# Bias tables beside the first image, tail loads on ScalarE's queue, image sums every two pairs

## What is computed

```
x = x + windowed_attention(group_norm(x))         # windows of 8x8, shifted by 4; 8 heads; relative bias table
t = tokens(x)                                      # 1024 a image
t = t + banded_attention(layer_norm(t))            # windows of 128 tokens, band of 32; 4 heads
t = t + experts(layer_norm(t))                     # top 2 of 8 experts: gelu(x W1 + b1) W2 + b2
```

## Time and profile before

| what | us |
|---|---|
| median of 3 runs | 3270.21 |
| lowest and highest run | 3255.96 and 3283.94 |
| the profiled execution | 3266.06 |
| its span, first to last instruction | 3264.20 |
| passes end, last pairs begin (about) | 2828 |

### The profile page before, as it was taken

The page is one execution under the profiler, slowest core; times in us unless marked ns, Lnnn a source line. Parts: engine busy times, 40 slices in busy tenths (PEclk is TensorE's granted clock), DMA queues, the critical chain, the costliest instruction groups (busy, mean ns, idle before and its releaser), DMA issues.

```text
span 3264.2 us, 76818 instructions
## 1 busy us (share of the span) xinstructions
PE 2561.1 (78%) x27338; PEld 1806.2 (55%) x27338; DVE 1947.2 (60%) x5091; ACT 1863.9 (57%) x3409; POOL 1778.5 (54%) x2054
## 2 busy tenths in 40 slices
PE   3888888888888888788999888989888777545460
PEld 1455555556666666566666666666665555434340
DVE  2467777777666666767666776667766655312122
ACT  1576565566776677567766777777766554212120
POOL 0335555555444444666666666666677775443336
PEclk9899999998999999899999999999998888778775
DMA  3343333433444544334334353343433344444543
GB/s 110 117 159 115 116 114 112 158 147 130 152 158 167 174 162 143 106 92 121 121 121 121 95 157 109 113 117 117 137 120 111 109 130 122 140 126 153 160 146 91
DMA packets 262426, 421.97 MB, mean 129 GB/s; under 512 B 41741, under 2 KB 141081, under 8 KB 261281
## 3 DMA queue, kind: packets, MB, share of 16 engines
q1 hardware_dynamic: 229280, 349.88, 32.3%
q0 software_dynamic: 32768, 67.17, 7.3%
HBM read 198.26 MB, written 231.22 MB: 132 GB/s over the span
## 4 chain that ended last, share of the span: by engine, by line
PE 30%; ACT 9%; issue 8%; another core or an unknown queue 4%; POOL 4%; DVE 4%; SPq 1%; DMA 1%; ACTq 0%; POOLq 0%; DVEq 0%
PE bank_m L824 6%; PE bank_m L817 4%; POOL yg L1215 2%; PE bank_to L751 2%; PE bank_s L706 2%; PE bank_s L719 2%; PE bank_s L745 1%; PE bank_s L797 1%; PE bank_s L791 1%; PE bank_to L760 1%; ACT pt_sb_a L1035 1%; ACT v_a L1020 1%; ACT L1162 1%; PE bank_s L729 1%
## 5 line engine op out<-in xcount | busy, mean ns | idle before, releaser
L1215 POOL DMA_INDIRECT yg<-y_sorted,place_i x512 | 511.9, 1000 | 434.2 <-DMA out_dram<-yg 119.7
L1205 POOL DMA_INDIRECT x_sorted<-xn_c,place_i x512 | 532.3, 1040 | 322.2 <-PE bank_s L690 121.2
L1198 POOL TENSOR_TENSOR s_sb_a<-s_sb_a,mx_a 128x512 f32<-128x512 f32 x256 | 266.9, 1043 | 614.4 <-DVE mx_a L1557 608.8
L1549 DVE TENSOR_TENSOR s_sb_a<-bank_s,bias_a 128x512 f32<-128x512 f32 x256 | 176.7, 690 | 447.9 <-PE bank_s L690 267.2
L817 PE MATMUL bank_m<-xe,wk_e 128*128 128x512 f32 x552 | 277.3, 627 | 62.8 <-ACT hid L1068 46.0
L824 PE MATMUL bank_m<-wk_e,hid 128*128 128x128 f32 x2208 | 290.8, 296 | 3.3 <-ACT hid L1068 3.3
L824 PEld LDWEIGHTS bank_m<-wk_e,hid 128*128 128x128 f32 x2208 | 285.3, 212 | 4.4 <-issue 4.3
L1198 POOL TENSOR_TENSOR s_sb_b<-s_sb_b,mx_b 128x512 f32<-128x512 f32 x256 | 269.4, 1052 | 23.8 <-DVE mx_b L1557 23.6
L1035 ACT ACTIVATE pt_sb_b<-bank_to 128x512 f32<-128x512 f32 x256 | 152.6, 596 | 207.1 <-PE bank_to L751 127.2
L1189 POOL TENSOR_TENSOR km_a<-qk_a,k_consts 128x128 f32<-128x128 f32 x512 | 207.7, 429 | 79.3 <-DVE qk_a L1401 74.7
L1068 ACT ACTIVATE hid<-bank_m,wk_e 128x512 f32<-128x512 f32 x276 | 182.3, 686 | 94.5 <-PE bank_m L817 62.3
(11 more groups left out here) (220 smaller groups left out, 6053.4 us busy)
## 6 DMA issues: line engine op xcount, KB each, us to landing
y_sorted<-t_back SPq DMA_DIRECT2D x192, 512.0 KB
wk_e<-in_w_experts_dram SPq DMA_DIRECT2D x156, 321.0 KB
y_sorted<-yo SPq DMA_DIRECT2D x170, 256.0 KB
xs<-x_sorted SPq DMA_DIRECT2D x156, 256.0 KB
t_kept<-t SPq DMA_DIRECT2D x64, 256.0 KB
t_back<-t_kept SPq DMA_DIRECT2D x32, 512.0 KB
xin<-in_x_dram SPq DMA_DIRECT2D x128, 112.0 KB
x_res<-in_x_dram SPq DMA_DIRECT2D x256, 56.0 KB
```

The costliest lines, as they stand in the source:

```text
L1198: pool.tensor_tensor(s[:, :, :], s[:, :, :], m[:, :, None].to_broadcast(shape), ALU.subtract).then_inc(s_sub[w], 1)
L1205: pool.indirect_dma_start(out=x_sorted[group_of[d] % XSIDES].ap(), out_offset=bass.IndirectOffsetOnAxis(ap=place_i[:, d, n:n + 1], axis=0) ...
L1215: pool.indirect_dma_start(out=yg[:, c % 2, n, :], out_offset=None, in_=y_sorted[side].ap(), in_offset=bass.IndirectOffsetOnAxis(ap=place_i ...
L1549: tt(s_sb[0][:, :, :].rearrange("p (r h) n -> p r (h n)", h=2), scores, bias_a[:, kind, :, :].rearrange("p (r h) n -> p r (h n)", h=2), AL ...
```

## The change

Three things are changed.

1. The start. The loads are split: six that the table needs (`table_loads`, semaphore `table_loaded`) come first, then the first image, then the 14 others (`loads`, semaphore `loaded`). SyncE sends the table out and back ahead of the 12 zero stores. TensorE no longer waits for `ready` or for the table's return; the 16 unfolding matmuls are done in two halves inside pass -1, at t = 4 behind the keys' projection and at t = 5 behind the squared norms. VectorE splits the rows behind step 5 of pass -1 and makes the four tables behind its step 7. TensorE waits for both in step 0 of pass 0, behind its first scores. The banks that the table uses in PSUM are others.
2. The loads of the tail. From pair 2 of the tail on, `load_pair` is called by ScalarE, behind the Gelus of pair n and the copy of pair n+1, instead of by SyncE ahead of the store of pair n.
3. `PAIRS_PER_SUM` is 2.0: images 20 to 27 are summed behind pairs 2, 4, 6, 8, 10, 14, 16 and 18, and 28 to 31 late.

The core of the diff:

```diff
-PAIRS_PER_SUM = 2.5
+PAIRS_PER_SUM = 2.0
...
+        table_loads = [(tab_s, rel_table), (cw1_s, cpb_w1), (cb1_s[:], cpb_b1),
+                       (cw2_s[:], cpb_w2.rearrange("(c p) n -> p c n", p=P)), (fold_s, unfold), (k[:], consts)]
+        loads = [(wq_s[:], wq), (wk_s[:], wk), (wv_s[:], wv), (wo_s[:], wo),
...
+        def load_pair(eng, u):
...
             load_image(0)
+            for dst, src in loads:
+                sp.dma_start(dst, src).then_inc(loaded, 16)
+            sp.wait_ge(setup, RELS)
+            sp.dma_start(scratch.ap(), rel_s).then_inc(bias_io, 16)
+            sp.wait_ge(bias_io, 16)
+            unfolded = bass.AP(scratch, 0, [[1, WS], [REL, HA * REL], [1, WS]])
+            sp.dma_start(unf_s, unfolded).then_inc(bias_io, 16)
             sp.wait_ge(blank, 1)
             for side in range(XSIDES):
...
-            sp.wait_ge(setup, 9)
-            sp.dma_start(scratch.ap(), rel_s).then_inc(bias_io, 16)
...
             for n, u in enumerate(tail):
-                if n + 2 < len(tail):
-                    load_pair(tail[n + 2])
                 store_pair(u)
...
# TensorE
-            pe.wait_ge(loaded, 16 * len(loads))
+            pe.wait_ge(table_loaded, 16 * len(table_loads))
...
-            pe.wait_ge(ready, 3)
+            pe.wait_ge(loaded, 16 * len(loads))
+            mm(T[:, 0:P], cols[:, 2:3].to_broadcast([P, P]), wo_s[:], start=True, stop=True).then_inc(rows_split, 1)
+
+            def unfold_table(rows):
+
+                pe.wait_ge(bias_io, 32)
+                for py in rows:
+                    last = mm(bank_m[:, 0, :].rearrange("p (h n) -> p h n", h=HA), fold_s[:, py * P:py * P + P],
+                              unf_s.rearrange("p (h y) w -> p h (y w)", h=HA)[:, :, py * WS:py * WS + WTOK],
+                              start=(py == 0), stop=(py == WS - 1))
+                if rows[-1] == WS - 1:
+                    last.then_inc(setup, 1)
...
+                if n == 0:
+                    pe.wait_ge(rows_split, SPLIT)
+                    pe.wait_ge(setup, BIASED)
...
+                if t == 4 and i == -1:
+                    unfold_table(range(0, WS // 2))
                 if t == 5 and on(f):
                     squared_norms(f, (0, 1))
+                if t == 5 and i == -1:
+                    unfold_table(range(WS // 2, WS))
# ScalarE, the tail
                 if n + 1 < len(tail):
                     slots_copy(pairs[tail[n + 1]], tail_banks[(n + 1) % 4])
+                if n >= 0 and n + 2 < len(tail):
+                    load_pair(act, tail[n + 2])
# VectorE
+            def output_rows():      # the split of two rows, as before, on rows_split
...
+            def window_bias():
+
+                dve.wait_ge(setup, UNFOLDED)
+                for kind in range(4):
+                    a = CONST["mask_a"][0] + kind * WTOK
+                    last = tt(bias_a[:, kind, :, :], bank_m[:, 0, :].rearrange("p (h n) -> p h n", h=HA),
+                              k[:, None, a:a + WTOK].to_broadcast([P, HA, WTOK]), ALU.add)
+                last.then_inc(setup, 1)
+                dve.wait_ge(setup, BIASED)
...
             for i in range(-1, PASSES):
                 for t in range(TILES):
                     step(i, t)
+                    if i == -1 and t == 5:
+                        output_rows()
+                if i == -1:
+                    window_bias()
```

More of the change, by code:

```diff
@@ L443, in hybrid_kernel @@
                  (row_b, b_proj.to_broadcast([P, P])), (bo_s, bo.to_broadcast([P, P])),
[L444 to L445 removed]
+                 (gb_s[:], gate_b.to_broadcast([P, E]))]
+        RELS, UNFOLDED, BIASED, SPLIT = 7, 8, 9, 17
+        def load_pair(eng, u):
+            pair = pairs[u]
+            side, tiles = pair.group % XSIDES, table[pair.group % 2]
+            if u == 0 or pairs[u - 1].group != pair.group:
+                eng.wait_ge(tabled, TABLE_STEPS * (pair.group + 1))
+                eng.wait_ge(scattered, 16 * TOP * TILES * (last_image[pair.group] + 1))
+                eng.wait_ge(zeroed, 16 * (SPARE_DMAS + E * pair.group))
+                zeros = x_sorted[side].ap()[E * REGION:E * REGION + SLOTS, :].rearrange("(p j) d -> p (j d)", p=P)
+                for e in range(E):
+                    row = eng.value_load(tiles[0:1, 2 * MAX_TILES + e:2 * MAX_TILES + e + 1],
+                                        min_val=0, max_val=BUFFER - SLOTS)
+                    rows = x_sorted[side].ap()[bass.ds(row, SLOTS), :].rearrange("(p j) d -> p (j d)", p=P)
+                    eng.dma_start(rows, zeros).then_inc(zeroed, 16)
+                eng.wait_ge(zeroed, 16 * (SPARE_DMAS + E * (pair.group + 1)))
+            for m, q, kth in pair.members:
+                b = buffer_of(q)[0]
+                after(eng, yo_ready, q - (3 if q < TAIL_FIRST else 5))
+                if b >= 4:
+                    eng.wait_ge(s_ready[0], IMAGES * TILES)
+                    eng.wait_ge(km_ready, IMAGES * TILES)
+                row = eng.value_load(tiles[0:1, kth:kth + 1], min_val=0, max_val=BUFFER - SLOTS)
+                expert = eng.value_load(tiles[0:1, MAX_TILES + kth:MAX_TILES + kth + 1], min_val=0, max_val=E - 1)
+                rows = x_sorted[side].ap()[bass.ds(row, SLOTS), :].rearrange("(p j) d -> p (j d)", p=P)
+                eng.dma_start(xs_b[b], rows).then_inc(tile_in[b], 16)
+                weights = w_experts[bass.ds(expert, 1), :, :].rearrange("e p n -> (e p) n")
+                eng.dma_start(wk_b[b], weights).then_inc(tile_in[b], 16)
@@ L464, in load_residual @@
                                      x_rolled[a, r, c0:c1, tiles, :]).then_inc(xr_in[h], 16)
[L466 to L486, removed]
-                    row = sp.value_load(tiles[0:1, kth:kth + 1], min_val=0, max_val=BUFFER - SLOTS)
-                    expert = sp.value_load(tiles[0:1, MAX_TILES + kth:MAX_TILES + kth + 1], min_val=0, max_val=E - 1)
-                    rows = x_sorted[side].ap()[bass.ds(row, SLOTS), :].rearrange("(p j) d -> p (j d)", p=P)
-                    sp.dma_start(xs_b[b], rows).then_inc(tile_in[b], 16)
-                    weights = w_experts[bass.ds(expert, 1), :, :].rearrange("e p n -> (e p) n")
-                    sp.dma_start(wk_b[b], weights).then_inc(tile_in[b], 16)
             def store_pair(u):
```

100 lines of the change are left out of this document (42 added, 58 removed).

## The result

| kernel | median us | runs | ratio to the kernel before, 95% interval |
|---|---|---|---|
| before | 3269.12 (3255.96 to 3283.94) | 4 | |
| changed | 3224.61 (3209.92 to 3239.77) | 4 | 0.9859 [0.9817, 0.9902] |
| changed, measured once more (before: 3265.62) | 3230.84 (3223.49 to 3244.22) | 6 | 0.9896 [0.9865, 0.9926] |

The change makes the kernel faster by 1.0 to 1.4%, 35 to 45 us (each median against that of the kernel before in the same runs, 3269.12 and 3265.62). Its first profile is of an execution of 3209.92 us, 14.7 under its own median, so it flatters the change; the second profile, of the same program, has a span of 3225.7. I read both, since the two together show what in one profile is chance.

The account below looks back on a forecast made before the run. Bound: a TensorE pipeline with waits, so gains only at the ends: a serial start, and GpSimd's gathers last. 3266.06 - 38.1 (start) - 2 (end) = 3226, or 3230 against the median; range 3205 to 3262.

Parts of the forecast that it names:

- Start, forecast 38.1 saved (28.3 to 41.1): Start: transposes 41.1 us earlier, less 3.0 us because the unfolding now stands in the first image's way.
- the cover of 8 us: Start: the table is back at 21.1 us and wanted only at 29.5, so its return delays nothing.
- since the clock was granted in full there: Start: reason for assuming fast unfolding matmuls, making the values' matmuls 3.0 us late, not 12.8.
- rival (d): Start: the unfolding's matmuls stay at the slow interval, so only 28.3 us are saved, total 3240; chance 0.13.
- End, forecast -2 (-17 to +14): Tail: sums -3.6, slower loading +5, later group switch +3.5, weight waits saved -7; net -2 us.
- The cadence term (+5): Tail: with ScalarE's loads a steady pair takes 9.0 us instead of 8.36, over some eight pairs, +5 us.
- The group switch: Tail: the switch to group 5 starts on ScalarE behind a copy, later than on SyncE, +3.5 us.
- two fifths: Tail: share counted as gain, -7 us, of TensorE's 18.9 us of weight waits outside the group switch.
- (b): Tail: all waits for weights are won and one more gather stretch takes in a pair, -14 us, 3216; chance 0.18.
- (c): Tail: ScalarE's late issue keeps a pair out of two gather stretches, +16 us, total 3246; chance 0.22.
- (e): Tail: ScalarE's issue creeps beside gathers and holds the Gelus past six stretches, +88 us, total 3320; chance 0.05.
- the two signs of being wrong: Passes not beginning 38 us earlier; GpSimd's 119.7 us of store waits at the end changing by over 15.

Follow-up runs that it names:

- the start alone: Kernel before with only the new start; the tail's loads stay on SyncE and sums come every 2.5 pairs: 3235.34 us, ratio 0.9882.
- the sums alone: Kernel before with only PAIRS_PER_SUM set to 2.0, old start and loads on SyncE: 3273.32 us, ratio 1.0008.
- loads alone: Kernel before with only the tail's loads moved to ScalarE's queue, old start, sums every 2.5 pairs: 3269.32 us, ratio 0.9995.
- 2.5 pairs: Changed kernel with PAIRS_PER_SUM put back to 2.5, new start and ScalarE's loads kept: 3224.86 us, ratio 0.9869.
- one unfolding matmul: Changed kernel with the table's unfolding as one matmul of 64 rows instead of 8 of 8 rows: 3236.30 us, ratio 0.9913.
- loads put back: Changed kernel with the tail's loads back on SyncE ahead of each pair's store: 3244.36 us, ratio 0.9913.

## Why the prediction was right

The time was forecast at 3230 and came at 3224.6 and 3230.8. The mechanism was right: the start alone measures 0.9882 and the two parts of the tail 1.0008 and 0.9995 by themselves. That the number was hit so closely is in part luck, since the start gave less than its 38.1 in every profile.

*Start, forecast 38.1 saved (28.3 to 41.1).* Measured 30.4 and 36.7. The transposes stood at 15.45 (forecast 15.0). The table was ready on VectorE at 14.1 (13.1), and went out at 14.13; the way back was issued at 15.46, so the way out took 1.3 us where it had taken 4.7 (issues at 25.71 and 30.43) behind 12 stores of zeros. TensorE shows no wait for the table's return: the cover of 8 us held. A half of the unfolding took 3.7 us (3.5), and the values' matmuls were 41.12 - (78.28 - 40.7) = 3.5 us late (3.0) in the second profile. The step that was only half right is "since the clock was granted in full there". These rows can't carry it: the profile gives 1.00 for the kernel before's 8-row matmuls too, which ran at the slow interval. In the nine profiles with the new start and 8-row matmuls the first scores stand between 46.2 and 53.0, so the start gave 30 to 37 us and never 38.1. In four of them (46.2 to 46.6) TensorE keeps the fast interval up to 41 us; in five (49.4 to 53.0) it falls to the slow one under the unfolding or the norms. The lowest of these, 30, is near rival (d)'s 28.3. Of (d)'s reason a part is refuted and a part is open. Eight rows aren't slow by themselves: where the clock was full they took 0.46 us. In the kernel before the 128-row projection behind them began at the slow interval as well (3.54 us for its first four, at 65.30, and 1.88 for the next). But 14 us of them on end did not bring TensorE to the fast interval there, and whether they let it fall here no run decides; in the profile of the sums alone, with the old start, it fell under the norms, where no 8-row matmul is near, and the scores came at 86.3 for 83.1.

*Passes, forecast unchanged.* No cause for a change was found. The two profiles have the same 26,420 matmuls and differ by 18 us, and so does TensorE's busy time (stretches from the first scores to the last scatter, first profile and second):

```profile
53.00:2797.00 2744.00, 2333.87 (x26420) 1655.18 (x26408) 1852.51 (x4964) 1781.56 (x3296) 1587.91 (x1854) 0.94 0.40 130
```

```profile
46.00:2808.00 2762.00, 2353.60 (x26420) 1673.31 (x26420) 1850.99 (x4964) 1783.72 (x3298) 1594.34 (x1854) 0.93 0.40 129
```

They take 19.7 us less where the mean granted clock is 0.94 than at 0.93. The 14 profiles of this document go the same way: their passes run from 2744.6 us at a mean clock of 0.939 (the changed kernel's first profile, the shortest of all) to 2776.0 at 0.927, though the passes' code is the same in each. So the first profile's 56.1 us hold 20.6 us from the passes that were not forecast, and lack 7.7 of the start's.

*End, forecast -2 (-17 to +14).* Measured -5.1 and +1.2. GpSimd's idle time, which all terms together move, became 3.9 and 0.1 shorter. It went away before images 23 and 28 (24.7 and 12.7 before) and came back before 25 and 29, and before 22, which was to start as before (32.6, now 40.0 and 41.1). That last one comes with the loads. In the five profiles that have them on ScalarE (changed twice, loads alone, 2.5 pairs, one unfolding matmul) the pause before image 22 is 40.0 to 41.1 us, and the copies of `xe` begin again 53.4 to 53.7 us after the last scatter; in the four that have them on SyncE (before, start alone, sums alone, loads put back) it is 32.6 to 33.8, and they begin at 48.2 to 50.0. The forecast had no term for these 7 us; shorter pauses later made up for them. The cadence term (+5) was too large: copies of `xe` were 8.5 apart, not 9.0, so that eight steady pairs cost about 1 us. The group switch: TensorE's wait for weights there was 14.7 and 15.5 where it had been 9.4, +5 to +6 for +3.5. All other waits for `wk_e` fell from 18.9 to 3.5 and 5.0, by 14 to 15 where two fifths were counted. In all they are 18.2 and 20.5, not under 15, and 14.7 and 15.5 of that is the switch. That GpSimd's idle time is nearly the same in spite of it fits the reason for counting little, a stretch of gathers right behind; it isn't shown. The sum of the terms is nothing, as forecast, and the loads alone (0.9995) and sums alone (1.0008) say so with narrower intervals. That the loads alone gained nothing on a second queue (0.9995) agrees with the Trainium skill, "DMA: Bandwidth & Descriptors", section "Issuing engines are not separate DMA queues".

*Rivals.* (b), 14 us from the end, and (c), 16 us of lost pairs, fall by the ends measured, -5.1 and +1.2. (e)'s mechanism exists: beside gathers, ScalarE's issues of one pair ran from 3027.72 to 3046.00, and its next Gelu came at 3049.18.

```profile
3027.72 0.34 ACTq L474 DMA_DIRECT2D xs<-x_sorted  x1
3028.22 0.96 ACTq L476 DMA_DIRECT2D wk_e<-in_w_experts_dram  x1
3041.09 0.70 ACTq L474 DMA_DIRECT2D qk_a<-x_sorted  x1
3045.29 0.71 ACTq L476 DMA_DIRECT2D qk_a<-in_w_experts_dram  x1
3049.18 1.26 ACT L1079 ACTIVATE hid<-bank_s,wk_e 128x512 f32<-128x512 f32 x2 [21.66 <-remote]
```

The loads alone (0.9995) show that it cost nothing to speak of; that a pair beside gathers stands anyway is the likely reason. The argument against (e) had a slip: a copy at 2927.44 leaves 13.6 us to 2941, less than the 14.7 that the issue takes, so it should not "just be over in time". Small ones change nothing: two fifths of 18.9 are 7.6 and not 7, slow halves are 7.0 us and not 6.8 (14.02 / 2), and the end's lower bound of -17 has no working.

*The signs.* Of what was to show it right, these came: the transposes (15.45), the unfolding at 0.46 us in the second profile, VectorE's first addition without a wait for the bias, and an earlier start of the gathers of 23 and 24 in the first profile (of 23 alone in the second). Missed were the scores at 45 (52.7 and 46.4), copies 9.0 apart (8.5) and waits for weights under 15. Of the two signs of being wrong, the first came by its letter, since the passes began 30.4 and 36.7 us earlier and not 38. The second did not: the waits for an image's store, rightly sorted, are 13.6 and 3.3 us shorter.

*What I took as given.* That the pairs stand until a stretch of gathers is over, for a reason the trace doesn't tell: this was the largest thing in the tail, 106 us of pairs, and I left it out of the sum because both kernels have it. For the forecast that was right. For the kernel it was where the time lay.

## What to carry to other kernels

When a part of a pipeline stalls beside another and the trace doesn't say why, slow the other one down by a known amount: here memsets of 0.97 us between gathers of 0.95 us gave the kernel before 1.2%, as much as the whole change under study, and both together 1.9%. Work that nothing needs until later can leave the head of a kernel at three quarters of its length or more (41 us at the transposes gave 30 to 37 at the first scores), but the stretch it moves into has a clock of its own. Take a second profile of the same program before a difference of 18 us in the passes, or 6 in a tail, is given a cause. And where an instruction waits for several semaphores, look in the kernel for the one that was still needed: here the profile's name for a wait moved 100 us from one cause to another, and the wait had not changed.

## What the runs showed of the hardware

Beside gathers at full rate, one each 1.25 us, all other engines can stand still at once. In the stretch from 2936.4 to 2956.1 of the first profile:

```profile
2942.25 1.88 PE L822 MATMUL bank_s<-xe,qk_a 128*128 128x512 f32 x4
...
2942.56 0.34 ACTq L474 DMA_DIRECT2D xs<-x_sorted  x1
...
2943.45 0.01 ACTq L476 DMA_DIRECT2D wk_e<-in_w_experts_dram  x1
2943.92 0.94 POOL L1228 DMA_INDIRECT yg<-y_sorted,place_i  x1 [0.30 <-issue]
...
2955.16 0.94 POOL L1228 DMA_INDIRECT yg<-y_sorted,place_i  x1 [0.30 <-issue]
2956.23 0.69 DVE L1547 TENSOR_TENSOR yo<-bank_m,wk_e 128x512 f32<-128x512 f32 x1 [14.86 <-remote]
```

The last matmul starts at 2943.54, and from there to 2956.23, for 12.7 us, no engine but GpSimd starts anything and no other DMA is issued. VectorE is the first to go on, 0.13 us after the last gather's end, with a result whose matmuls are in the records up to 2942.4. Such holes, of over 4 us from one start to the next on any engine or queue but GpSimd's, which end behind the last scatter with a pair's `yo` or Gelu:

| kernel | holes | us |
|---|---|---|
| before | 5 | 52.1 |
| changed, first and second profile | 7 and 4 | 87.2 and 64.7 |
| with 16-column memsets | 6 | 64.8 |
| with 1,024-column memsets, changed and before | 1 and 1 | 10.6 and 7.9 |
| each gather after the landing of the one before | 1 | 8.5 |

The hole that is left in each slowed kernel lies at or right behind the last scatters, which are not slowed; their other long pauses end with VectorE's sum, when its gathers have landed. The longest holes are the first ones, beside images 20 and 21 (33 and 36 us in the two profiles of the changed kernel); in the kernel before that hole (29 us) ended 10 us before the gathers did, so they don't always last to a stretch's end. What it is that stands still, the signals between the engines, their instructions or their access to memory, no run here tells. That the time from one gather to the next decides, and not an instruction between them, is shown by three rates: at 1.25 to 1.5 us the holes are there, with and without a short memset; at 2.1 to 2.2 us (long memset) and 3.1 us and more (no memset) they are not.

From the issue of the table's transfer to the chip's memory to the issue of the one that waits for it, it took 1.3 us ahead of the stores of zeros (14.13 to 15.46) and 4.7 behind them (25.71 to 30.43).
